# Attention slots of an audio tower reordered: query halves two slots apart, probability copies ahead of reciprocals, value products last

## What is computed

```python
x = layernorm(h)                                   # (64, 128, 64)
q = x @ wq.T                                       # 16 heads of 64
k, v = split(x @ wkv.T)                            # one head of 64
q = rmsnorm(rope(q), q_norm_w); k = rmsnorm(rope(k), k_norm_w)
scores = where(mask, q @ k.T / 8, -1e30)
attn = softmax(scores)
h = h + (attn @ v) @ wo.T
```

## Time and profile before

| | us |
|---|---|
| runs of before, median (lowest to highest) of 3 | 2319.99 (2319.36 to 2320.64) |
| the profiled execution's own time | 2317.79 |
| its span | 2316.0 |
| PE busy | 2077.2 (90%) |
| DVE busy | 1682.9 (73%) |
| ACT busy | 1470.6 (63%) |
| POOL busy | 777.3 (34%) |

### The profile page before, as it was taken

How to read it: one execution, slowest core, us unless ns; L and a number is a source line. 1 busy time by engine, 2 the same in 40 slices (tenths; PEclk the granted TensorE clock), 3 DMA queues, 4 the chain that set the end, 5 groups by cost and what they waited for, 6 DMA issues and landing times. The chain is left out here.

```text
span 2316.0 us, 35857 instructions
## 1 busy us (share of the span) xinstructions
PE 2077.2 (90%) x10589; PEld 1492.2 (64%) x10661; DVE 1682.9 (73%) x3691; ACT 1470.6 (63%) x3736; POOL 777.3 (34%) x1413
## 2 busy tenths in 40 slices
PE   4999999999999977999958888888888888877999
PEld 3788888888888865877735555555555555544554
DVE  4677787787787765566558888888888888864555
ACT  1466656666666643444438888888888888863554
POOL 0111211112112110132256555655556555534100
PEclk9999999999999998999969999999999999997999
DMA  3000000000000000000000000000000000000000
GB/s 111 11 7 7 6 10 6 6 9 6 6 9 6 0 0 1 1 1 1 1 0 1 1 1 1 1 1 1 1 1 1 1 1 1 1 1 3 12 10 14
DMA packets 14447, 15.24 MB, mean 7 GB/s; under 512 B 9995, under 2 KB 10251, under 8 KB 14051
## 3 DMA queue, kind: packets, MB, share of 16 engines
q1 hardware_dynamic: 14307, 13.58, 2.0%
HBM read 11.48 MB, written 2.10 MB: 6 GB/s over the span
## 5 line engine op out<-in xcount | busy, mean ns | idle before, releaser
L1416 ACT ACTIVATE apb<-ps,anb,arq 128x128 f32<-128x128 f32 x1024 | 455.9, 461 | 104.2 <-DVE anb L1290 103.6
L1524 POOL TENSOR_TENSOR apb<-apb,arc 128x512 f32<-128x512 f32 x256 | 266.5, 1041 | 236.5 <-DVE arc L1299 236.5
L1169 PE MATMUL ps<-akT,aqT 128*128 128x256 f32 x1024 | 263.5, 380 | 8.8 <-issue 2.5
L1284 DVE TENSOR_REDUCE amx<-ps 128x4 f32<-128x512 f32 x256 | 175.1, 684 | 97.9 <-PE ps L1169 97.3
L1180 PEld LDWEIGHTS ps<-const,apb 128*128 128x128 f32 x1024 | 112.4, 141 | 178.3 <-issue 106.5
L1416 ACT ACTIVATION_READ_ACCUMULATOR apb<-ps,anb,arq 128x1 f32 x1024 | 211.5, 207 | 0.0
L117 PE MATMUL ps<-h0h,w123h 128*128 128x512 f32 x512 | 207.2, 405 | 3.4 <-POOL h0l L602 1.7
L1169 PEld LDWEIGHTS ps<-akT,aqT 128*128 128x128 f32 x1024 | 196.3, 192 | 21.3
L1518 POOL TENSOR_TENSOR aqr<-at 128x512 f32<-128x512 f32 x128 | 163.4, 1277 | 127.1 <-DVE at L1245 127.1
L119 PE MATMUL ps<-h0h,w123l 128*128 128x512 f32 x512 | 202.8, 396 | 0.0
L1180 PE MATMUL ps<-const,apb 128*128 128x128 f32 x1024 | 162.5, 281 | 44.8 <-POOL apb L1524 43.9
(11 more groups left out here) (303 smaller groups left out, 5317.5 us busy)
## 6 DMA issues: line engine op xcount, KB each, us to landing
x<-in_x SPq DMA_DIRECT2D x32, 176.0 KB
out<-fyo SPq DMA_DIRECT2D x16, 128.0 KB, 1.9
w<-in_w SPq DMA_DIRECT2D x1, 1024.0 KB, 7.8
mw<-in_mw SPq DMA_DIRECT2D x1, 1024.0 KB, 9.6
const<-in_const SPq DMA_DIRECT2D x1, 612.0 KB
wqkv<-in_wqkv SPq DMA_DIRECT2D x1, 576.0 KB, 9.7
fw<-in_fw SPq DMA_DIRECT2D x1, 512.0 KB, 8.3
fsel<-in_fsel SPq DMA_DIRECT2D x1, 512.0 KB, 7.9
```

Source lines behind the costliest of these rows:

```text
L1169: last = pe.matmul(bank[:, p * 2 * T:(p + 1) * 2 * T], qT[:, i % 2, 2 * k + p, :], kT[:, i // 4 % 2, i % 4, :, :].rearrange("p a s -> p (a ...
L1284: ve.tensor_reduce(mx[:, k, :], ps[:, SB[n % 3], :].rearrange("p (h s) -> p h s", h=4), AX_X, ALU.max).then_inc(S["mx"], 1)
L1416: last = ac.activation(pb[:, i % 2, head, :], ps[:, SB[n % 3], h * T:(h + 1) * T], ACT.Exp, bias=nb[:, k, h:h + 1], scale=rq[:, i % 2, hea ...
L1524: po.tensor_tensor(p, p, rc[:, i % 2, 4 * k:4 * k + 4].unsqueeze(2).to_broadcast([T, 4, T]), ALU.mult).then_inc(S["pn"], 1)
```

## The change

In TensorE's stream the value product becomes the last call of a slot instead of the second. Projections go to j = 3 (first half, a clip further ahead) and j = 1 (second half), two slots apart, and the query transposes to j = 1 and 3; VectorE's rope and GpSimd's sum of the halves move with the projections, ScalarE's square and copies with them too. `rms_q` gets a table of its own (j = 3). In VectorE's slot the copy of the transposed probabilities goes ahead of the reciprocal. The maximum is written negated, and the product becomes a plain `tensor_tensor` multiplication in place of the `scalar_tensor_tensor`. The key transpose moves from slot 10 to 12 of a quad, `w_o` from 3 to 6 to 4 to 7, `turn` from 8 to 9, `residual` from 8 to 10, `statistics` from 9 to 12; the slot range is two longer.

```diff
-    at_kt = by_slot(QUADS, lambda q: first(q) + 10)
-    at_q = by_slot(HALVES, lambda m: 4 * (m // 2 - 1) + m % 2)
-    at_qt = by_slot(HALVES, lambda m: 4 * (m // 2 - 1) + 2 + m % 2)
+    at_kt = by_slot(QUADS, lambda q: first(q) + 12)
+    at_q = by_slot(HALVES, lambda m: 4 * (m // 2) - 5 + 2 * (m % 2))
+    at_qt = by_slot(HALVES, lambda m: 4 * (m // 2) - 3 + 2 * (m % 2))
+    at_rms = by_slot(B, lambda i: 4 * i - 1)
...
-    at_wo = {16 * (q + 1) + 3 + c: (q, c) for q in range(QUADS) for c in range(4)}
-    at_tr = by_slot(QUADS, lambda q: 16 * (q + 1) + 8)
-    SLOTS = range(first(0) - 4, max(at_tr) + 2)
+    at_wo = {16 * (q + 1) + 4 + c: (q, c) for q in range(QUADS) for c in range(4)}
+    at_tr = by_slot(QUADS, lambda q: 16 * (q + 1) + 9)
+    SLOTS = range(first(0) - 4, max(at_tr) + 4)
...
                 for u in SLOTS:
                     if 0 <= u < PARTS:
                         scores(u)
-                    if u in at_pv:
-                        p_v(at_pv[u])
                     if u in at_pt:
                         p_t(at_pt[u])
...
                     if u in at_tr:
                         turn(at_tr[u])
+                    if u in at_pv:
+                        p_v(at_pv[u])
...
-                    ve.tensor_reduce(mx[:, k, :], ps[:, SB[n % 3], :].rearrange("p (h s) -> p h s", h=4), AX_X, ALU.max
-                                     ).then_inc(S["mx"], 1)
+                    ve.tensor_reduce(mx[:, k, :], ps[:, SB[n % 3], :].rearrange("p (h s) -> p h s", h=4), AX_X, ALU.max,
+                                     negate=True).then_inc(S["mx"], 1)
...
-                    ve.scalar_tensor_tensor(out=nb[:, k, :], in0=mx[:, k, :], scalar=-1.0,
-                                            in1=rq[:, i % 2, 4 * k:4 * k + 4], op0=ALU.mult, op1=ALU.mult
-                                            ).then_inc(S["nb"], 1)
+                    ve.tensor_tensor(nb[:, k, :], mx[:, k, :], rq[:, i % 2, 4 * k:4 * k + 4], ALU.mult
+                                     ).then_inc(S["nb"], 1)
...
                     if 0 <= u < PARTS:
                         maximum(u)
+                    if u in at_pt:
+                        p_copy(at_pt[u])
                     if 0 <= u - 1 < PARTS:
                         recip(u - 1)
-                    if u in at_pt:
-                        p_copy(at_pt[u])
...
-                    if u in at_tr:
-                        residual(at_tr[u])
                     if u - 1 in at_tr:
-                        statistics(at_tr[u - 1])
+                        residual(at_tr[u - 1])
+                    if u - 3 in at_tr:
+                        statistics(at_tr[u - 3])
...
                         keep_q(at_qt[u - 1])
-                        if at_qt[u - 1] % 2 == 0:
-                            rms_q(at_qt[u - 1] // 2)
+                    if u in at_rms:
+                        rms_q(at_rms[u])
```

## The result

| | before | after |
|---|---|---|
| median (lowest to highest), us | 2320.31 (2319.36 to 2321.23), 4 runs | 2305.01 (2301.66 to 2305.94), 4 runs |
| span of the profiled execution | 2316.0 | 2299.8 |
| a quad (16 slots) | 54.41 | 53.19 in 12, 54.8 in 2 (the first, without `w_o`, 49.0) |

The ratio is 0.9931 (95% interval 0.9914 to 0.9949): faster by 0.7%, 15 us, where 51 was forecast, and outside the range of 2225 to 2300. The profiled execution is the fastest of the four (2301.66).

A forecast was written before the change was run, and what follows sets the result against it. No engine is full; the latency of a PE, DVE, POOL round, 6.03 us per two slots, bounds it. Pairs sum to 50.95 against 54.41 a quad, 15 x 3.4 = 51 us less: 2269, own range 2240 to 2300, stated 2225 to 2300.

The forecast's parts named there:

- 15, 0 (`x_t`): 6.0 each: Quad's sum, slots 15 and 0 with the next quad's input transposes: the pair takes 6.0 us.
- POOL keeps its order, only the sums come two slots apart: POOL's queue: order unchanged by the edit, counted among the parts costed at nothing.
- slots 1, 2: Quad's sum, pair with `k_v` on PE: scores and copy about 0.1 late, 6.25 us, between 6.0 and 6.5.
- The circle: Steady slots, PE transposes, DVE copy and reciprocal, POOL normalization, next transposes: 6.03 us for two slots, against PE's 5.02.
- 9, 10: Quad's sum, pair where weighing the keys holds slot 9's product: 0.4 on the copy, 6.4 us.
- plain pairs of 6.03: Two slots without the quad's own work: hops between engines add up to 6.03 us, PE waiting about 1.0.
- if the quad is above 53, a hop of the circle was too short: Sign to check: a 16-slot quad above 53 us, where near 51 was forecast, means an underestimated hop.
- The reciprocal behind the copy at nothing: VectorE's slot: waiting for exponentials adds 0 per pair, bounds 0 to the 1.15 us seen before.
- The plain product is held as the old one: VectorE's plain multiplication still waits for GpSimd's work to end; change of operation taken as 0.
- Rival A: VectorE's plain product escapes POOL's hold: some 5.6 us a pair, 94 us less, 2226; chance 0.12.
- The clock: Attention stretch: granted clock 1.00 (2.4 GHz), no part of the bound, and stays 1.00.
- Later key and output steps at nothing: `w_o`, `turn`, `k_t`, residual and statistics in later slots: due a quad later, so costed at nothing.

The follow-up runs named there:

- the kernel of 2246.2: The changed kernel with GpSimd's row steps one slot earlier and the reciprocal again ahead of the copy: 2246.24 us, ratio to before 0.9693.
- 2265.49: The changed kernel with row steps one slot earlier, reciprocal ahead of the copy and value product second again: 2265.49 us, ratio to before 0.9772.
- 2264.62: The kernel before with only the query steps two slots apart and the row steps one slot earlier: 2264.62 us, ratio to before 0.9772.

## Why the prediction was wrong

**The step that failed** is one term of the quad's sum, "15, 0 (`x_t`): 6.0 each". I moved the half-query sum into slot 15 on POOL and costed what it holds on VectorE, but not what is queued behind it on its own engine: the last row step, for which TensorE's `x_t` and, behind that, slot 0's exponentials wait. I wrote "POOL keeps its order, only the sums come two slots apart"; in slot 15 there had been no sum. The pair measured 3.08 + 5.06 = 8.1. Taking the step away gave 27 us back, and 2277.68 is 9 above the forecast of 2269 and well inside its own range. Those 9 lie around the same slot: with the rows earlier the pair 15, 0 still takes 6.44 where I had 6.0, and slots 1, 2 take 6.63 where I had 6.25. What those 0.8 are is open.

**The circle.** Pair by pair, forecast and measured distance of maxima in the kernel after: slots 1, 2: 6.25, 6.43; 3, 4: 6.5, 6.55; 5, 6: 7.0, 7.03; 7, 8: 6.5, 6.16; 9, 10: 6.4, 6.92; 11, 12: 6.0, 6.27; 13, 14: 6.3, 5.67. The seven sum to 44.95 forecast and 45.03 measured. That the sum is so near is partly luck, since single pairs are off by up to 0.6: the product in slot 9 lasted 0.94, a hold of 0.78 where I had 0.4, and slots 11 to 14 sum to 11.94, no more than two plain pairs of 6.03, though they hold the statistics. My own sign, "if the quad is above 53, a hop of the circle was too short", would have misled: the quad was 53.19 and the hops were right in the sum.

**The reciprocal behind the copy at nothing.** Wrong as a cost of the edit, though not in the total: the 0.59 stands in my circle. I weighed only the cover (waits for exponentials, 0 to 1.15) and didn't ask what the circle would be without the edit. It costs 23 us in the changed kernel, 31 with the rows moved, and alone on the kernel before 6 by the median, of which its profile shows at most 2.4 in the steady slots. Nor was "one waited 1.15 us" the whole of the wait that it covers: it was 21.9 us in 30 waits. The size that I gave the wait behind the edit, nothing, was right (0.4 us in the kernel after).

**The plain product is held as the old one.** Right, by the traces of both operations and the run with the old one. It bears out the Trainium skill, "SBUF — State Buffer", section "SBUF: two separate sides", for a plain tensor product: in the kernel after, the product of 1571.81 took 0.68 and ended at 1572.49, POOL's sum at 1572.47. Rival A put an escape from the hold at 43 us beyond the forecast (94 against 51). No kernel here has such an escape; taking the product away altogether, in the kernel of 2246.2, gave 35 us.

**Value product last, queries apart.** Right in sign, not in the sum. Alone they are worth 23.6 and 39.6 us on the kernel before, and the copy first costs 6.1 by the medians: together 57, the change 15. What is lost between is `x_t`'s wait, which the value product had partly filled (0.59 with it in front, 1.52 without), and the copy's step on the circle: undoing the two gave 59.

**The clock.** I wrote that it is no part of this. In the kernel after it fell in two quads, 1.65 us each; the wait that preceded it was the one I had missed. **Later key and output steps at nothing:** right by the medians (2265.49 against 2264.62).

## What to carry to other kernels

When a step moves to another slot, list on its own engine what now stands behind it and who waits for that, in every slot of the longest period and not only in the short one. An order that protects one wait (the copy ahead of the reciprocal) can lengthen the circle, here by 1.7 us a quad; once other edits have removed the wait, try the old order again. Edits that each win alone have to be tried together: here the query slots alone win 40 us and the whole change 15. Before reading a small difference of medians as an edit's price, look where in the span it lies: of the 8.8 us between the profiles of the copy-first kernel and the kernel before, 6.2 lay outside the slots that the edit was meant for. And ask of each step on the circle whether the output needs it: a softmax doesn't need the exact row maximum, and that step was worth 35 us.

## What the runs showed of the hardware

A single wait of TensorE of 1.52 us between packed slots was followed in some quads (2 of 14 in the kernel after) by a stretch at 1.2 GHz that cost 1.65 us, and in the others by none. With the old product the same wait was followed by it in 5 of 14, and with the row steps earlier no quad of the steady stretch shows it. It is probably one reason why the runs of these two kernels spread: their profiled executions, with two and with five such quads, took 2301.66 and 2307.66.

A product of VectorE with two inputs in SBUF, four numbers in each partition, took 0.16 us free and up to 0.94 (1.18 in the kernel before) while GpSimd worked, and the plain and the three-operand form did so alike.

The 16 output products of the last quad took 3.65 us in the kernel before and 5.85 in the copy-first kernel, where most of them ran at a granted clock of 0.50.
